# Attention loop of an audio tower: PE's blocks in another order, values projected for eight heads at a time

## What is computed

```python
h = tok(x)                       # windows of 8 frames, two relu layers, batch norm: (32, 93, 256)
n = layernorm(h)
q, k, v = (einsum('bsm,hmd->bhsd', n, kernel[i]) for i in range(3))     # 16 heads of 64
attn = softmax(einsum('bhsd,bhtd->bhst', q, k) * scale)
h = h + reshape(einsum('bhst,bhtd->bhsd', attn, v)) @ WO                # feature order (d, h)
n = layernorm(h)
probs = softmax(n @ router_w);  top 2 of 8 experts
h = h + shared(n) + sum(gate * expert_e(n)) + n                         # 256 -> 1024 gelu -> 256
```

## Time and profile before

| | |
|---|---|
| median of 3 runs | 1137.86 us (1135.79 to 1140.1) |
| profiled execution | 1141.44 us, its span 1139.8 us |
| PE busy | 1058.8 us, 93% of the span, 9140 matmuls |
| DVE busy | 619.8 us, 54% |
| ACT busy | 527.3 us, 46% |
| POOL busy | 420.7 us, 37% |
| granted PE clock, mean | 0.979 of full speed |

### The profile page before, as it was taken

One profiled execution on the slowest core, in us unless ns is written; L12 is line 12 of the kernel. 1 busy time (PEld: TensorE's weight loads), 2 busy tenths in 40 slices (PEclk: granted clock), 3 DMA queues, 4 the chain that ended last, 5 costly groups with the idle time before them and its releaser, 6 DMA issues. The chain is left out here.

```text
span 1139.8 us, 26472 instructions
## 1 busy us (share of the span) xinstructions
PE 1058.8 (93%) x9140; PEld 1007.2 (88%) x9141; DVE 619.8 (54%) x1692; ACT 527.3 (46%) x1309; POOL 420.7 (37%) x505
## 2 busy tenths in 40 slices
PE   5994999999999999999999699999999999998998
PEld 5993889898888888989888699999999999998898
DVE  3665656767677676767756755233243332332454
ACT  3542445444544544454444455454454544544252
POOL 2000223234252523435252322423664264153882
PEclk9997999999999999999999799999999999999999
DMA  9517990001000100100011243313331312311553
GB/s 187 122 34 246 353 346 17 29 19 37 8 20 27 27 27 18 36 9 18 27 25 59 95 114 130 120 37 120 120 111 45 120 58 98 120 46 42 158 141 110
DMA packets 81571, 99.05 MB, mean 87 GB/s; under 512 B 29968, under 2 KB 64496, under 8 KB 81520
## 3 DMA queue, kind: packets, MB, share of 16 engines
q1 hardware_dynamic: 57648, 58.87, 17.2%
q0 software_dynamic: 18176, 29.12, 8.8%
q10 hardware_dynamic: 5696, 10.39, 2.7%
HBM read 50.48 MB, written 47.74 MB: 86 GB/s over the span
## 5 line engine op out<-in xcount | busy, mean ns | idle before, releaser
L1225 POOL TENSOR_TENSOR prob<-prob,rc 93x372 f32<-93x372 f32 x128 | 103.2, 807 | 332.7 <-DVE rc L1119 332.1
L853 PE MATMUL pj_ps<-xg,wA 128*128 128x372 f32 x768 | 153.1, 347 | 4.2 <-DVE next_row L774 2.8
L1708 DVE TENSOR_TENSOR act_s<-dn_ps,act_s 128x256 fp32r<-128x256 f32 x112 | 47.6, 425 | 199.6 <-ACT act_s L1587 199.6
L853 PEld LDWEIGHTS pj_ps<-xg,wA 128*128 128x128 f32 x768 | 131.0, 192 | 10.3 <-DVE next_row L774 3.4
L841 PE MATMUL pj_ps<-wB,xg 128*93 128x256 f32 x768 | 105.8, 286 | 0.0
L1108 DVE TENSOR_REDUCE mx<-s_ps 93x4 f32<-93x372 f32 x128 | 67.0, 524 | 63.7 <-PE s_ps L866 63.7
L983 ACT ACTIVATE qT<-pj_ps 128x372 f32<-128x372 f32 x64 | 30.8, 482 | 146.5 <-PE pj_ps L853 144.9
L841 PEld LDWEIGHTS pj_ps<-wB,xg 128*93 128x93 f32 x768 | 91.8, 159 | 7.0
L899 PE MATMUL y_ps<-wB,oT 128*124 128x256 f32 x576 | 88.3, 297 | 2.2 <-DVE oT L1123 1.8
L1483 PE MATMUL up_ps<-rx,wB 128*128 128x256 f32 x720 | 86.4, 278 | 4.1 <-ACT act_s L1587 2.5
L1483 PEld LDWEIGHTS up_ps<-rx,wB 128*128 128x128 f32 x720 | 83.9, 188 | 5.5 <-ACT act_s L1587 3.1
(11 more groups left out here) (175 smaller groups left out, 2096.2 us busy)
## 6 DMA issues: line engine op xcount, KB each, us to landing
slots<-zeros SPq DMA_DIRECT2D x8, 3072.0 KB, 23.1
rows_in<-slots SPq DMA_DIRECT2D x29, 256.0 KB, 2.6
raw<-in_L_ffn_routed_up POOLq DMA_DIRECT2D x7, 1024.0 KB, 5.4
raw<-in_L_ffn_routed_down POOLq DMA_DIRECT2D x7, 1024.0 KB, 8.3
slots<-rows_out ACTq DMA_DIRECT2D x28, 256.0 KB, 2.0
ln_out<-split SPq DMA_DIRECT2D x8, 744.0 KB
frames<-in_x SPq DMA_DIRECT2D x8, 400.0 KB
raw_w<-in_L_attn_kernel SPq DMA_DIRECT2D x6, 512.0 KB, 5.4
```

The lines of the kernel that those rows point to most:

```text
L853: ins = pe.matmul(pj_ps[:, t, 0:N], wA[:, wp, at:at + P], xg[:, dp, m, :], start=(k == 0), stop=(k == 5))
L1225: pool.tensor_tensor(p, p, rc[:, u % 2, :].unsqueeze(2).broadcast_to([TP, 4, SL]), ALU.mult).then_inc(scaled, 1)
L1708: dve.tensor_tensor(act_s[:, LO, f, 0:ET], act_ps[f % 2], act_s[:, HI, f, 0:ET], ALU.subtract).then_inc(ract_lo, 1)
```

## The change

1. **v for eight heads.** `VW` goes from 256 to 512 columns: a v tile serves four pairs instead of two, and there are 8 tiles in a group instead of 16. They stand in steps 0, 1, 2, 3, 5, 7, 9 and 11, one each. `v_rows` doubles.
2. **output behind q and k.** `output(j)` moves from the end of step 2j+5 to step 2j+6, behind that step's q and k and ahead of its turn. In steps 13 and 14 it is no longer cut in two.
3. **rank, q0, k0** of step 15 stand at the step's head, in this order, ahead of the turn (before: turn, q0, output, rank, k0).
4. The second row tile moves to step 2, logits from step 11 to step 10 ahead of the turn.
5. On ACT and DVE the matching steps move: `take_logits` to step 10, `add`, moments and x_rows one step later, z_rows from step 11 to 12, routing one step earlier with the masks in step 14, `take_ranks` to the head of step 15. POOL's root steps begin one head later.

The diff, cut to its core:

```diff
@@ -494,7 +494,7 @@
         raw2_in = sem(ctx, "raw2_in")
         with ExitStack() as c:
             NU = 2 * NJ
-            VW = 2 * P
+            VW = 4 * P
             xg = sb(c, "xg", [P, 2, MC, N], F32R)
             qT = sb(c, "qT", [P, 2, N])
             kT = sb(c, "kT", [P, 2, N])
@@ -534,11 +534,10 @@
 
             def tiles(kind):
                 ahead, behind = kind != "last", kind != "first"
-                t = ["q1", "k1", "v00", "v01", "v02", "v03"] + ["p10", "p11"] * ahead + ["q2", "k2", "v10", "v11", "q3", "k3"]
-                t += ["v12", "v13", "q4", "k4", "v20", "v21", "q5", "k5", "v22", "v23"]
-                t += ["z20", "z21"] * behind + ["q6", "k6", "v30", "v31"] + ["logits"] * behind + ["q7", "k7", "v32", "v33"]
-                t += ["z10", "z11"] * ahead + ["rank"] * behind + ["q0", "k0"] * ahead
-                return t
+                t = ["q1", "k1", "v00", "v01"] + ["p10"] * ahead + ["q2", "k2", "v02"] + ["p11"] * ahead + ["v03", "q3", "k3"]
+                t += ["v10", "q4", "k4", "v11", "q5", "k5", "v12"] + ["z20", "z21"] * behind + ["q6", "k6"]
+                t += ["logits"] * behind + ["v13", "q7", "k7"] + ["z10", "z11"] * ahead + ["rank"] * behind
+                return t + ["q0", "k0"] * ahead
 
             def bank_of(tile):
                 if tile[0] in "vz":
@@ -875,16 +874,16 @@
                     ins.then_inc(turned, 1)
 
                 def values(g, j):
-                    if j % 2 == 0:
+                    if j % 4 == 0:
                         for b in range(2, 4):
-                            pe.wait_ge(taken[b % 2], number(g, "v%d%d" % (j // 2, b)))
+                            pe.wait_ge(taken[b % 2], number(g, "v%d%d" % (j // 4, b)))
                     pe.wait_ge(turned_out, g * NU + 2 * (j + 1))
                     ge(pe, o_lo, g * NJ + j)
                     for b in range(GB):
                         cols = slice(b * TP, (b + 1) * TP)
                         for h in range(2):
-                            at = (j % 2) * P + h * DH
-                            ins = pe.matmul(o_ps[h * DH:(h + 1) * DH, cols], v_rows[:, (j // 2) % 2, b, at:at + DH],
+                            at = (j % 4) * P + h * DH
+                            ins = pe.matmul(o_ps[h * DH:(h + 1) * DH, cols], v_rows[:, j // 4, b, at:at + DH],
                                             probT[:, (2 * j + h) % 4, cols], start=True, stop=True)
                     ins.then_inc(pv_done, 1)
 
@@ -903,7 +902,7 @@
                         ins.then_inc(wo_done, 1)
 
                 def group(g, behind, ahead):
-                    V = {0: "00 01", 1: "02 03", 3: "10 11", 5: "12 13", 7: "20 21", 9: "22 23", 11: "30 31", 12: "32 33"}
+                    V = {0: "v00", 1: "v01", 2: "v02", 3: "v03", 5: "v10", 7: "v11", 9: "v12", 11: "v13"}
                     for s in range(NU):
                         if s > 0 and s % 2 == 0:
                             scores(g, s // 2)
@@ -912,41 +911,36 @@
                             if s == 0:
                                 scores(g, 0)
                             qk_tile(g, "k%d" % (s // 2 + 1))
-                        for v in V.get(s, "").split():
-                            v_tile(g, "v" + v)
+                        if s % 2 == 0 and s >= 6:
+                            output(g, s // 2 - 3)
+                        elif s % 2 == 0 and behind:
+                            output(g - 1, NJ + s // 2 - 3)
+                        if s == 10 and behind:
+                            logits_tile(pe, g, g - 1)
+                        if s in V:
+                            v_tile(g, V[s])
+                        if s == NU - 1 and behind:
+                            rank_tile(pe, g, g - 1)
+                        if s == NU - 1 and ahead:
+                            pe.wait_ge(taken[1], number(g, "z11"))
+                            qk_tile(g, "q0")
+                            qk_tile(g, "k0")
                         if s >= 2:
                             turn(g, s - 2)
                         elif behind:
                             turn(g - 1, NU + s - 2)
-                        if s == 1 and ahead:
-                            rows_tile(pe, g, 0, g + 1)
+                        if s in (1, 2) and ahead:
+                            rows_tile(pe, g, s - 1, g + 1)
                         if s == 9 and behind:
                             back_tile(pe, g, 1, 0, g - 1, x_rows)
                             back_tile(pe, g, 1, 1, g - 1, x_rows)
                         if s == 13 and ahead:
                             back_tile(pe, g, 0, 0, g + 1, z_rows)
                             back_tile(pe, g, 0, 1, g + 1, z_rows)
-                        if s == NU - 1 and ahead:
-                            pe.wait_ge(taken[1], number(g, "z11"))
-                            qk_tile(g, "q0")
                         if s % 2 == 0 and s >= 4:
                             values(g, s // 2 - 2)
                         elif s % 2 == 0 and behind:
                             values(g - 1, NJ + s // 2 - 2)
-                        if s in (13, 14):
-                            output(g, 4, range(0, 2) if s == 13 else range(2, C))
-                        elif s % 2 and s >= 5:
-                            output(g, (s - 5) // 2)
-                        elif s in (1, 3) and behind:
-                            output(g - 1, NJ - 2 + s // 2)
-                        if s == NU - 1 and behind:
-                            rank_tile(pe, g, g - 1)
-                        if s == NU - 1 and ahead:
-                            qk_tile(g, "k0")
-                        if s == 1 and ahead:
-                            rows_tile(pe, g, 1, g + 1)
-                        if s == 11 and behind:
-                            logits_tile(pe, g, g - 1)
 
                 def start():
                     rows_tile(pe, -1, 0, 0)
@@ -962,6 +956,7 @@
 
                 def drain():
                     g = NG - 1
+                    output(g, NJ - 3)
                     turn(g, NU - 2)
                     values(g, NJ - 2)
                     turn(g, NU - 1)
@@ -1018,7 +1013,7 @@
                     act.activation(oT[:, j % 2, HI, :], o_ps[:, 0:N], ACT.Copy).then_inc(o_hi, 1)
 
                 def group(g, behind, ahead):
-                    V = {0: "00", 1: "02", 3: "10", 5: "12", 7: "20", 9: "22", 11: "30", 12: "32"}
+                    V = {0: "00", 2: "02", 5: "10", 9: "12"}
                     for s in range(NU):
                         if s % 2 == 0 and s // 2 + 1 < NJ:
                             take_q(g, s // 2 + 1, g)
@@ -1031,8 +1026,8 @@
                             take_turned(g, s - 2)
                         elif behind:
                             take_turned(g - 1, NU + s - 2)
-                        if s == 1 and ahead:
-                            take_rows(act, g, 0, g + 1)
+                        if s in (1, 2) and ahead:
+                            take_rows(act, g, s - 1, g + 1)
                         if s == 9 and behind:
                             hi(act, g, 1, 0, g - 1)
                             hi(act, g, 1, 1, g - 1)
@@ -1124,16 +1117,18 @@
 
                 def routing(s, place, n):
 
-                    plan = {12: ("max", "shift", ""), 13: ("sum", "recip", "scale top"), 14: ("", "", "index expert"),
-                            15: ("", "masks both", "pick slots")}
+                    plan = {11: ("max", "shift", ""), 12: ("sum", "recip", "scale top"), 13: ("", "", "index expert"),
+                            14: ("", "masks both", ""), 15: ("", "", "pick slots")}
                     for step in plan.get(s, ("", "", ""))[place].split():
                         route(dve, n, step)
 
                 def group(g, behind, ahead):
-                    V = {0: "01", 1: "03", 3: "11", 5: "13", 7: "21", 9: "23", 11: "31", 12: "33"}
+                    V = {1: "01", 3: "03", 7: "11", 11: "13"}
                     for s in range(NU):
                         if s % 2 == 0:
                             shift(g, s)
+                        if s == NU - 1 and behind:
+                            take_ranks(dve, g, g - 1)
                         if behind:
                             routing(s, 0, g - 1)
                         if s >= 1:
@@ -1153,22 +1148,19 @@
                             take_o(g, s // 2 - 2)
                         elif s % 2 == 0 and behind:
                             take_o(g - 1, NJ + s // 2 - 2)
-                        if s == NU - 1 and behind:
-                            take_ranks(dve, g, g - 1)
-                        if s == 3 and behind:
+                        if s == 4 and behind:
                             add(g - 1)
                         if ahead:
-                            if s == 2:
+                            if s == 3:
                                 moments(dve, g, 0, g + 1)
-                            if s == 3:
```

(22 more changed lines are left out.)

8 lines of the change are left out of this document (3 added, 5 removed).

## The result

The changed kernel takes 1177.68 us (median of 4 runs, 1177.32 to 1182.38) against 1136.82 (4 runs, 1135.23 to 1140.1) of the kernel before beside it: ratio 1.0365, 95% interval 1.0329 to 1.0401. It is slower, as forecast, and the time lies in the range; but the forecast was +23 us and it is +41.

A forecast was written before the change was run, and what follows sets the result against it. PE's own stream was taken to bound the attention loop. Six middle groups +15, first -0.5, last +1 gave +15.5 us; the clock's +7.5 made +23, or 1161 us against the median of 1137.9, range 1143 to 1181.

The forecast's parts named there:

- (a): Step 11: PE idles before v13 until DVE frees the logits' bank behind take_o(3) and keep; 2.3 us a group.
- (b): Steps 12 and 13: PE waits at the back tiles for z rows normalised behind take_o(4); 2.1 us a group.
- (c): Step 15: rank asks for DVE's masks a step earlier, so PE waits 2.1 us, up to 2.5.
- (d): Step 0: PE waits because ACT takes k0 behind take_turned(13) and an exp; 0.35 us.
- Waits that go: Step 15's turn wait for POOL, next_row and step 7's wait vanish or are covered; 2.6 us a group saved.
- Output behind q and k: Output follows matmuls of its own number form; a pair takes 7.17 instead of 7.39, eight save 1.8 us a group.
- The rival by which like matmuls switch for nothing: Output after q and k: matmuls of one number form gain nothing, 1.8 us a group not won; 1174, chance 0.05.
- Values for eight heads: v tiles: 48 matmuls of 512 columns replace 96 of 256 a group; no gain, no loss, six taking 1.49 us.
- The clock: PE's clock falls after 9 of 14 new idle stretches, 1.2 us each; less 3.5 from before, +7.5 us.
- The fourth: Knock-on rival: every clock fall costs in full and (c) takes 2.5 us; +38.5, 1176, chance 0.17.
- The first: Rival: PE's clock holds through the new waits; +12, 1150 us, chance 0.15.
- The second: Rival, DVE's steps 12 to 14: DVE runs ahead, (b) and (c) do not show; -14, 1124, chance 0.07.

The follow-up runs named there:

- e2: The changed kernel with the z rows normalised in step 11, as before the change, instead of step 12; 1173.03 us, ratio 1.0315.
- e5: The changed kernel with each v tile made as two chains of 256 columns in the same bank; 1176.69 us, ratio 1.0352.
- e1: The changed kernel with DVE reading the logits ahead of take_o(3) and keep in step 10; 1154.34 us, ratio 1.0151.
- the fourth kernel: The changed kernel with logits read earlier, z rows in step 11, rank between q0 and k0, k0 copied ahead of turned rows; 1139.31 us, ratio 1.0029.
- e3: The changed kernel with scores(5) computed twice more where PE waits for the logits' bank; 1168.54 us, ratio 1.0259.

## Why the prediction was right, and short

The mechanism was right: the waits, their places and the gains. That the time lies in the range does not prove the sum, though: the clock's term was less than half of what it measured, and 6.4 us come from a stage that the sum did not have.

**Waits that come: right, each at its place.** (a) 2.20 us against 2.3; (b) 1.70 against 2.1; (c) 0.70 in the trace, 1.86 at the full clock, against 2.1; (d) 0.36 against 0.35. Together 6.1 at the full clock against 6.9. As a sum they hold; as prices for mending them one by one they do not, since e2 shows that (b) and (c) hang on one chain.

**Waits that go: right.** No turn of the middle groups waits for POOL, no tile for `next_row`. "The waits at the first row tile and at the x back tiles stay as long as they are" was off: they are 0.35 and 0.36 instead of 0.20 and 0.27, +0.25 a group.

**Output behind q and k: right for a pair, wrong in its count.** 7.15 against 7.17. But "eight pairs save 1.8 us a group" is six. One output stood behind q0 before the change already, and the one of step 14 has no q or k of its own step ahead of it: it stands behind scores (448.74 above). 6 x 0.22 is 1.3. The rival by which like matmuls switch for nothing has fallen with the 7.15.

**Values for eight heads: right.** Hardly a gain: 1.46 us a tile behind values and 1.39 behind output (0.232 a matmul) against 1.49, and the halves of e5 take 0.02 us a tile more. The estimate of 1.30 a tile from the Trainium skill (TensorE: Matmul & The Clock Gate, Back-to-back issue gap) lies under both; the measurement decides.

**A middle group without its clock:** 6.1 + 0.25 - 2.6 - 1.3 = +2.5, forecast +2.5, the second with waits taken 0.8 too long and gains 0.5 too large. Measured it is 71.7 - 66.4 = 5.3, less the 2.2 and 0.4 of low clock: +2.7. The groups of e1 agree: two whose only fall lies behind (b), where it moves rank by nothing, take 66.83 and 66.85 us, and with (a)'s 2.2 that is 69.05. The first group, forecast at -0.5, came out at -2.0; the low stretch of 3.41 us that it had before, from 162.3 us, is gone there.

**The clock: the term that was mis-sized.** "Of the other 14 I take 9 to be followed by such a fall", at 1.2 us each. In the middle groups every (a) was followed by one, and in five of six its stretch was 6.83 us, not 3.41. The five cost 2.6 us each (2.2 behind (a), 0.4 behind (b)), 13 together, and the first of the six, 73.26 us long, 4.4: 17.5, where +7.5 had been set for the whole kernel. Price and length came from the one stretch of the earlier trace rows, where the wait ahead was 1.75 us; the waits expected were longer. That trace has two more low stretches of 3.41 us in the attention, from 162.3 and from 227.2 us, behind waits of 1.07 and 1.30 us, while five groups kept the clock through 1.33: a wait of that length could go either way. That (b)'s falls are mostly covered by (c) was right. At the start, in a stage that the change does not touch, two blocks at the low clock were 1.3 us longer each and the first scores 2.3 us later; the fourth kernel does not have it (109.05).

**The experts: missing.** "Together +15.5 us, if the clock stays" had no term for code that nobody edited. It cost 6.4 us in the profile: some 3 for ACT's jump, and the rest came with the late `act_s`. Moving ACT's code back took 3.8 off the median. The forecast's 23, with the missing 6.4, 2.3 at the start, 10 of clock (17.5 instead of 7.5) and 1.2 for the six groups' +2.7 instead of +2.5, less the 1.5 and 0.4 by which the first and the last group did better, makes 41.

**Rivals.** The fourth (1176: clock in full, (c) 2.5 us) was nearest in time. Its mechanism holds for (a) alone: (b)'s falls cost 0.4 us, (c) was shorter than 2.5, and the rest of its price came from the experts. The first fell with the first low stretch behind (a). The second (DVE ahead of where I put it) fell: DVE is idle 26 us of a group and still late.

## What to carry to other kernels

An order that puts like matmuls together is worth its switches (here 0.2 us a pair) only where the moved instructions find their operands ready: first list, for each engine, what a moved instruction now stands behind, since three moves of DVE's work by a step or less cost 5.8 us of waits a group (2.20, 1.70 and 1.86) against 3.9 of gains. Where waits in a row hang on one late chain, mending the first alone hands most of its time to the next. And price an idle stretch of PE with its clock: here 2.2 us of wait cost 2.2 us more behind it, unless another wait took that up. And before a difference in an untouched stage is explained, look at how far that stage differs between profiles of kernels that have it alike: here by 5 us.

## What the runs showed of the hardware

- The clock's falls were locked to the group. Five middle groups in a row have 6.83 us at half the clock behind an idle stretch of 2.20 and 3.41 us behind one of 1.70; in e3, filling the first with redundant matmuls moved the fall to the next idle stretches. In the kernel before, the clock fell behind 1.07 and 1.30 us of idle time in two groups and held through 1.33 in five.
- The time of a loop's backward jump on ACT depends on where the loop stands in ACT's code: 155 or 237 ns with the same instructions, set by 37 instructions ahead of it. With the slow jump one matmul in a block of 48 comes some 60 ns late and the 23 behind it take 117 to 118 ns instead of 113 to 114; the whole is some 3 us longer (3.8 and 2.8 by the medians of two pairs of kernels).
- A wait that is already fulfilled is not free on PE's queue: 114 instructions of two such waits each made the idle time before the first matmul 19.2 us instead of 8.0, and 142 made it 22.2, so 28 more cost 3.0 us, 0.11 each.
